# First attention as one stream of slots over four turns, with stacked fp32r score operands and the product by values ahead of the turns

## The chip, the core and the metric

The kernel runs on one core of a Trainium2 chip. A core has TensorE (PE: matrix products and transposes into PSUM), VectorE (DVE), ScalarE (ACT), GpSimd (POOL) and SyncE (SP, which here only issues DMAs). The metric is the device time of one execution in microseconds, as a median of several.

## The reference

Two layers over x of 8 sequences by 256 tokens by 256 numbers. Only the attention of layer 0 is touched by the change:

```python
xn = _layernorm(x)
q = heads(xn @ wq.T + bq); k = heads(xn @ wk.T + bk); v = heads(xn @ wv.T + bv)   # 32 heads of 8 numbers
scores = jnp.einsum('bhqd,bhkd->bhqk', q, k) / np.sqrt(8)
attn = softmax(where(causal, scores, -inf), axis=-1)
s = einsum('bhqk,bhkd->bhqd', attn, v).transpose(0, 2, 1, 3).reshape(B, S, H) @ wo.T + bo
g = silu(ffn0(xn));  x = x + s * g        # ffn0: router over 8 experts, top 2, and a shared expert
```

A second layer (another attention with 16 heads of 128, and 16 experts with top 4) follows; its text does not change.

## The kernel before

All is fp32 unless said otherwise. The first attention works on the 2048 tokens in four **turns** (`TURNS`) of 512, that is two sequences each. A turn has 32 **slots** (`SLOTS`): a slot is two heads of one sequence; `bb` is the sequence, 16 slots each. Queries and keys lie with the heads' 8 numbers along the partitions, so that 32 partitions hold four heads. The queries are `qT`; the keys are kept four times in `kTm`, each copy masked so that one head of each four is left (`keys`, L772: one DVE instruction for each copy), and a score product contracts over 32 partitions, 24 of them with zeros.

A slot's work goes over three engines, and each handles its own list in program order:

- **PE**, per slot (`scores`, L624, L626 and L630): products of queries and keys of two heads (256 and 128 columns, on two different groups of 32 partitions), and the causal mask added by a bf16 product with the identity. Two PSUM banks hold a slot's scores and two slots' scores alternate, so that `scores(s)` waits for the exponentials of slot s-2. Then `turn` (L640): six 128 by 128 transposes of the probabilities of slot s-2, through banks 4 and 5; each bank must have been copied out before it is written again. On every second slot `pv` (L659, L662): the product with the values for slots s-4 and s-3, which needs the copies of their transposed probabilities.
- **DVE**, per slot: the largest score of each row (L839, 256 wide, and L841, 512 wide), and then two copies of transposed probabilities of slot s-2 out of PSUM (L780).
- **ACT**, per slot: four exponentials with sums (L742, L744).

Beside these (`beside`) come side jobs at certain slots: the projection of values (L561), router logits (L568), the turning of the next turn's normalised tokens (L246), and in the third turn the router's choice and ranks (DVE L357 to L497, PE L440 and L443). At a **turn's end** the stream stops. PE drains the last turns and products, and then does `turn_inverse` (L673: the softmax's inverse sums turned), the projections of queries and keys for the next turn (L550), and the output projection `project` (L684), while DVE does `normalise` (L793), `keys` (L772) and `keep_out` (L799) and ACT `copy_out` and `queries` (L710). A new turn starts with `scores` of slot 0 once queries and the first four masked keys are there.

Of the other engines: POOL clears two large areas at the start (L2221, L2227), normalises, and in the last turn issues the 32 indirect DMAs (L502) that spread the tokens over the experts' rows. SP loads the constants, 1 MB of the second layer's weights, the shared and the eight experts' weights (4.9 MB in one DMA) and writes zeros to `xg` in 7 DMAs of up to 2 MB (L2132), all by the middle of turn 0. Behind the attention `pe_blocks0` (from L881) begins with the experts' blocks.

## Time and profile before

| | us |
|---|---|
| median of 3 runs (1939.71 to 1941.13) | 1941.01 |
| profiled execution: its time, and its span | 1924.45, 1922.6 |
| first attention: first slot of turn 0 to first product of the experts | 27.11 to 418.83 |
| busy between 36 and 418.8 us: PE, DVE, ACT, POOL | 364.19, 292.80, 231.68, 33.94 |
| DVE side jobs between 36 and 420: inverse sums (L784, L786), `normalise` (L793), `keep_out` (L799) | 7.7, 5.4, 5.5 (all four turns) |
| the same: normalising (L216, L221, L226); masked keys (L772) | 7.6 (three turns); 17.8 (24 instructions) |
| the same: router's choice, ranks and owners (L357 to L497) | about 9.7 (once) |
| an fp32r product of 512 columns (L1371), mean of one | 0.419 |

The rest of the time is the experts of layer 0 (to about 540 us) and the second layer. A row of the timeline is: start in us, duration in us (of a merged run of `xN` instructions, from the first's start to the last's end), engine, line, operation, result and operands, and in square brackets how long the engine had been idle and what released it. An fp32 product shows as two PE instructions, so `x4` in L624 is two products. The end of a product is modelled and lies some tenths of a us behind the moment at which the next one can start: what a group costs PE is read from start to start.

### The profile page before, as it was taken

The numbers are of one execution on the slowest core, as the hardware profiler recorded it, in microseconds if no ns is written. First come the engines' busy times: TensorE is split into PE (matmuls) and PEld (weight loads), VectorE is DVE, ScalarE is ACT, GpSimd is POOL, SyncE is SP. The second block draws the span as 40 slices with busy tenths as digits, with TensorE's granted clock in tenths as the row PEclk, the third lists the DMA queues.
The fourth block names the chain that finished last, engine by engine and source line by source line (L and its number), as shares of the span: only waits on it lengthen the run. The fifth ranks groups of instructions, "written<-read, shape, count | busy, mean of one in ns | idle before, by whom it ended". The sixth has DMA issues, their size and how long they took to land.

```text
span 1922.6 us, 34586 instructions
## 1 busy us (share of the span) xinstructions
PE 1815.3 (94%) x11822; PEld 1443.5 (75%) x11822; DVE 1282.4 (67%) x2811; ACT 906.2 (47%) x2978; POOL 832.7 (43%) x919
## 2 busy tenths in 40 slices
PE   6999999999987999999999999999999997999986
PEld 4767666767765887788888888888888886777754
DVE  5678787863457788888676766667667664444467
ACT  3657564753433444445454455544545543444422
POOL 2000000320056665565767767777676773000066
PEclk9899999999999999999999999999999998999999
DMA  9600000123342000000000000000000223333344
GB/s 345 231 1 2 1 1 1 59 90 112 90 158 94 1 1 12 1 6 1 15 20 14 19 16 14 19 14 11 25 11 22 77 78 136 106 108 107 105 132 123
DMA packets 75907, 114.29 MB, mean 59 GB/s; under 512 B 9505, under 2 KB 65953, under 8 KB 73089
## 3 DMA queue, kind: packets, MB, share of 16 engines
q1 hardware_dynamic: 66416, 86.38, 13.6%
q0 software_dynamic: 9216, 25.18, 4.0%
q8 instruction: 75, 1.23, 0.3%
q10 hardware_dynamic: 144, 1.05, 0.1%
q14 instruction: 56, 0.45, 0.1%
HBM read 64.86 MB, written 47.71 MB: 59 GB/s over the span
## 4 chain that ended last, share of the span: by engine, by line
PE 77%; DVE 10%; POOL 5%; issue 3%; ACT 3%; DMA 2%; POOLq 0%; DVEq 0%; SPq 0%; ACTq 0%
PE ps L1356 11%; PE ps L1371 9%; PE ps L1443 5%; PE ps L1889 5%; PE ps L1397 4%; PE ps L640 4%; PE ps L624 3%; PE ps L1385 3%; PE ps L1384 3%; PE ps L1383 3%; PE ps L902 2%; POOL work L2084 2%; PE ps L1378 2%; PE ps L1906 2%; PE ps L1908 2%
## 5 line engine op out<-in xcount | busy, mean ns | idle before, releaser
L1356 PE MATMUL ps<-work,weights 128*128 128x256 f32 x1024 | 248.3, 386 | 1.1 <-DVE work L1629 1.1
L1371 PE MATMUL ps<-split 128*128 128x512 f32 x768 | 227.8, 419 | 0.0
L1356 PEld LDWEIGHTS ps<-work,weights 128*128 128x128 f32 x1024 | 186.4, 191 | 22.1 <-DVE work L1629 1.3
L1771 POOL TENSOR_TENSOR work<-work,rope 128x512 f32<-128x512 f32 x128 | 164.5, 1286 | 53.1 <-ACT work L1544 53.0
L1777 POOL TENSOR_TENSOR work<-work 128x512 f32<-128x512 f32 x128 | 164.4, 1284 | 5.0
L502 POOL DMA_INDIRECT xg<-work x96 | 96.9, 1009 | 153.1 <-PE ps L630 140.2
L2084 POOL DMA_INDIRECT work<-yg,work x64 | 62.4, 975 | 227.1 <-DMA yg<-work 207.3
L742 ACT ACTIVATE work<-ps,work 128x128 f32<-128x128 f32 x256 | 95.4, 373 | 124.3 <-DVE work L841 117.4
L1371 PEld LDWEIGHTS ps<-split 128*128 128x128 f32 x768 | 130.9, 190 | 24.6
L780 DVE COPY work<-ps 128x384 f32<-128x384 f32 x256 | 130.0, 549 | 8.5 <-PE ps L640 8.4
L1443 PE MATMUL ps<-weights,work 128*128 128x256 f32 x512 | 124.0, 386 | 2.5 <-ACT work L1600 2.5
L640 PE MATMUL ps<-ident,work 128*128 128x128 f32 x768 | 116.5, 283 | 8.1 <-DVE work L780 8.0
L1651 DVE TENSOR_TENSOR work<-ps,keep_w 128x384 f32<-128x384 f32 x128 | 65.4, 553 | 87.1 <-PE ps L1379 86.8
L744 ACT ACTIVATE work<-ps,work 128x256 f32<-128x256 f32 x256 | 122.4, 478 | 0.0
L2021 DVE SCALAR_TENSOR_TENSOR work<-work,ps 128x176 f32<-128x176 f32 (+1 forms) x95 | 35.0, 369 | 121.5 <-ACT work L1972 121.5
L1585 ACT ACTIVATE work<-ps,work 128x128 f32<-128x128 f32 x256 | 90.6, 366 | 51.4 <-PE ps L1385 51.1
L1443 PEld LDWEIGHTS ps<-weights,work 128*128 128x128 f32 x512 | 99.4, 195 | 16.8 <-ACT work L1600 3.1
L1664 DVE RECIPROCAL work<-ps 128x256 f32<-128x256 f32 x64 | 111.9, 1748 | 0.0
L1550 ACT COPY work<-ps 128x256 f32<-128x256 f32 x128 | 47.1, 368 | 130.3 <-PE ps L1371 130.3
L1889 PE MATMUL ps<-weights,work 128*128 x316 | 106.8, 461 | 0.2 <-ACT work L1966 0.2
L1383 PE MATMUL ps<-work 128*128 128x64 f32 (+1 forms) x512 | 97.3, 272 | 9.1 <-DVE work L1651 9.1
L640 PEld LDWEIGHTS ps<-ident,work 128*128 128x128 f32 x768 | 88.1, 145 | 22.8 <-issue 11.5
(236 smaller groups left out, 4508.8 us busy)
## 6 DMA issues: line engine op xcount, KB each, us to landing
work<-xg SPq DMA_DIRECT2D x118, 128.0 KB, 2.2
yg<-work SPq DMA_DIRECT2D x118, 128.0 KB, 1.7
xg<-work SPq DMA_DIRECT2D x6, 2048.0 KB, 17.8
weights<-in_w SPq DMA_DIRECT2D x8, 1024.0 KB, 9.4
weights<-in_f SPq DMA_DIRECT2D x8, 1024.0 KB, 5.1
weights<-in_f SPq DMA_DIRECT2D x1, 4864.0 KB, 16.0
work<-xn SPq DMA_DIRECT2D x32, 128.0 KB, 2.2
weights<-in_wo SPq DMA_DIRECT2D x1, 2048.0 KB, 8.6
```

What stands on the lines that cost most here:

```text
L640: last = pe.transpose(ps[:, 4 + hh, k * P:(k + 1) * P], prob[:, s % RING, hh, k * P:(k + 1) * P], ident[:, :])
L744: act.activation(pr[:, P:BLK], sc[:, 0:SEQ], ACT.Exp, bias=nmax[:, s % RING, 1, hh:hh + 1], accum_out=total[:, bb, 1, h:h + 1]).then_inc(e ...
L780: dve.tensor_copy(probT[:, s % RINGT, hh, :], ps[:, 4 + hh, 0:BLK]).then_inc(probT_ready.sem, 1)
L1356: last = pe.matmul(ps[:, 2, which * SEQ:(which + 1) * SEQ], w1(h, (which * KC + kc) * P, P), xT[:, kc, :], start=kc == 0, stop=kc == KC - 1)
L1371: last = pe.matmul(ps[:, 3, :], x1_split[:, xp, kc, c * P:(c + 1) * P], w_vg[:, n % 2, wp, kc, :], start=i == 0, stop=i == KC * len(TERMS) ...
L1383: pe.matmul(outs[0], left[:, 0:P], rhs[0], start=True, stop=True)
L1443: last = pe.matmul(ps[:, 7, c * D:(c + 1) * D], ogT[:, hh, c * P:(c + 1) * P], weights[:, W1O + h * D:W1O + (h + 1) * D], start=h == 0 and ...
L1664: dve.reciprocal(enz[:, n % 2, :, :].rearrange("p c n -> p (c n)"), ps[:, 0, SEQ:2 * SEQ])\
L1771: pool.tensor_tensor(qk[:, h % 4, :, :], raw[:, h % 2, :, :], rope[:, 0, :].unsqueeze(1).broadcast_to([P, 2, SEQ]), ALU.mult).then_inc(rot ...
L1777: pool.tensor_tensor(qk[:, h % 4, :, :], qk[:, h % 4, :, :], rot_s[:, h % 2, :, :], ALU.add)\
L1889: last = pe.matmul(ps[:, 2 + b % 2, 0:GUW], xb4T[:, b % 2, kc * P:(kc + 1) * P], experts1[:, bass.ds(offset[b] + kc * GUW, GUW)], start=kc ...
L2084: pool.indirect_dma_start(out=yk4[:, c % 2, k, :], out_offset=None, in_=yg1[:, :], in_offset=bass.IndirectOffsetOnAxis(ap=route1.index[:, ...
```

## The change

What it does, part by part:

- The four turns become **one stream** of 128 slots (`ALL`), numbered g. The slot number within a turn is still s. All that stood at a turn's end is now a side job at some s, mostly odd: `lower_bank` and `upper_bank` on PE, `beside` on ACT and DVE. The results of `turn_inverse` and `project` use banks 6 and 7.
- **Scores as fp32r products.** ACT writes the projected queries and keys whole (`act_heads`), and `split_heads` splits each into an upper part (rounded to fp32r) and a lower part (the rest). On DVE for turn 0, on POOL for turns 1 to 3. SP writes these to DRAM (`write_halves`: 16 DMAs of 256 KB in a turn) so that for each head the 32 rows are upper-upper, upper-lower, lower-upper and lower-lower parts of its 8 numbers (queries take the first word, keys the second), and loads **stacks** back (`load_stack`: 16 DMAs of 256 KB in a turn, one for two slots, in a ring of 5). A score product contracts over these 32 rows in fp32r. The masked keys `kTm` are gone.
- **The product by values** (`pv`) stands right behind a slot's scores and ahead of the turns; before, it stood behind the turns.
- The zeros to `xg` go in 15 parts of up to 1 MB, one behind each of 15 stack loads of turns 0 and 1; experts' and shared weights, and the second layer's first 1 MB, are loaded in turn 2. `out_bias` and the ranks move to other slots; some semaphores are used again later.

The diff, cut to its core:

```diff
+FIRST = 15, 17
+ALL = TURNS * SLOTS
+RINGQ = 5
+PROJ = 2 * KC
...
+        def split_heads(eng, t, n):
+            index, ring = t * PROJ + n, n % 2
+            eng.wait_ge(full_ready.sem, full_ready.at(t, n + 1))
+            if index >= 2:
+                eng.wait_ge(halves_written[ring], 16 * 4 * (index // 2))
+            eng.tensor_copy(halves[:, ring, 0, :], full[:, ring, :]).then_inc(upper_ready.sem, 1)
+            eng.wait_ge(upper_ready.sem, upper_ready.at(t, n + 1))
+            eng.tensor_tensor(halves[:, ring, 1, :], full[:, ring, :], halves[:, ring, 0, :], ALU.subtract).then_inc(lower_ready.sem, 1)
...
+            def lower_bank(t, s):
+                if s == 1 and 0 < t < TURNS - 1:
+                    pe.wait_ge(full_ready.sem, full_ready.at(t, PROJ))
+                    logits(6)
+                if s == 1 and t == TURNS - 1:
+                    pe.wait_ge(full_ready.sem, full_ready.at(t, PROJ))
+                    pe.wait_ge(pow_rows, 7)
+                    route0.pe_rank(pe, 6)
+                if s == 21 and t < TURNS:
+                    turn_inverse(t, 0)
+                if s == 23 and t < TURNS:
+                    project(t, 0)
+                if t < TURNS - 1:
+                    if s == 25:
+                        pe.wait_ge(s0_ready.sem, s0_ready.at(t, 1))
+                        values(0)
+                    if s == 27:
+                        pe.wait_ge(v_ready.sem, v_ready.at(t + 1, HPQ))
+                        heads(t + 1, 2, 6)
+                    if s == 29:
+                        pe.wait_ge(full_ready.sem, full_ready.at(t + 1, 3))
+                        heads(t + 1, 3, 6)
...
+                    if s == FIRST[routed]:
+                        pe.wait_ge(norm0.xT_ready.sem, norm0.xT_ready.at(t + 1, 2))
+                        if routed:
+                            pe.wait_ge(lg0_copied.sem, lg0_copied.at(t + 1, 1))
+                        heads(t + 1, 0, 7)
+                    if s == FIRST[routed] + 2:
+                        pe.wait_ge(full_ready.sem, full_ready.at(t + 1, 1))
+                        heads(t + 1, 1, 7)
...
+            def scores(g):
+                n = g // 2
+                if g % 2 == 0:
+                    pe.wait_ge(stack_loaded[n % RINGQ], 16 * (n // RINGQ + 1))
+                if g >= 2:
+                    pe.wait_ge(exp_done.sem, exp_done.at(0, 2 * g - 2))
+                heads = [(2 * (g % 2) + hh, stack[32 * r:32 * r + 32, n % RINGQ, 0, :], stack[32 * r:32 * r + 32, n % RINGQ, 1, :])
                          for hh, r in enumerate(rows)]
 
                 for bank, q, k in heads:
-                    pe.matmul(ps[:, bank, 0:SEQ], q[:, q0 + P:q0 + SEQ], k[:, q0:q0 + SEQ], start=True, stop=True)
+                    pe.matmul(ps[:, bank, 0:SEQ], q[:, P:SEQ], k[:, 0:SEQ], start=True, stop=True)
...
-            for s in range(SLOTS + LAG + 1):
-                if s < SLOTS:
-                    scores(s)
-                    beside(s)
+            pe.wait_ge(norm0.xT_ready.sem, norm0.xT_ready.at(0, KC))
+            for n in range(PROJ):
+                heads(0, n, 2 + n)
+            values(0)
+            pe.wait_ge(consts_loaded, NCONST)
+            pe.wait_ge(bias_done, 5)
+            for g in range(ALL + 9):
+                t, s = divmod(g, SLOTS)
+                if g < ALL:
+                    scores(g)
+                if LAG < g <= ALL + LAG and (g - LAG) % 2 == 0:
+                    pv(g - LAG - 2)
+                lower_bank(t, s)
+                upper_bank(t, s)
                 for hh in range(2):
-                    if LAG <= s < SLOTS + LAG:
-                        turn(s - LAG, hh)
-                if s > LAG and (s - LAG) % 2 == 0:
-                    pv(s - LAG - 2)
...
+        def act_heads(act, t, n, bank):
+            which, mt = n % 2, n // 2
+            index = t * PROJ + n
+            act.wait_ge(proj_done.sem, proj_done.at(t, n + 1))
+            if index >= 2:
+                act.wait_ge(lower_ready.sem, lower_ready.at(0, index - 1))
+            act.activation(full[:, n % 2, :], ps[:, bank, :], ACT.Identity, bias=(bqs, BK)[which][:, mt:mt + 1],
+                           scale=(HD0 ** -0.5, 1.0)[which]).then_inc(full_ready.sem, 1)
...
-            def keys(turn, mt):
-                dve.wait_ge(k_done.sem, k_done.at(turn, mt + 1))
-                for j in range(HPQ):
-                    dve.tensor_scalar(kTm[:, j, mt, :], ps[:, 4 + mt, :], BK[:, mt:mt + 1], MASK[:, j:j + 1], ALU.add, ALU.mult)\
-                       .then_inc(keys_ready.sem, 1)
...
+            for g in range(ALL + 9):
+                if g < ALL:
+                    largest(g)
+                beside(*divmod(g, SLOTS))
+                if LAG <= g < ALL + LAG:
+                    copy_probs(g - LAG)
...
+            def write_halves(t, n):
+                which, mt, ring = n % 2, n // 2, n % 2
+                sp.wait_ge(lower_ready.sem, lower_ready.at(t, n + 1))
+                at = (t * KC + mt) * HPQ * P
+                rows = heads_by_part[at:at + HPQ * P, which * CH:(which + 1) * CH].rearrange("(h a b d) t -> a b h d t", a=2, b=2, d=HD0)
+                for a in range(2):
+                    for b in range(2):
+                        sp.dma_start(rows[a, b], halves[:, ring, (a, b)[which], :].bitcast(F32)).then_inc(halves_written[ring], 16)
+
+            def load_stack(n):
+                t, i = divmod(n, STACKS)
+                bb, mt, j = i // (KC * HPQ), i // HPQ % KC, i % HPQ
+                for w in range(2):
+                    sp.wait_ge(halves_written[w], 16 * 4 * (t * KC + mt + 1))
+                if n >= RINGQ:
+                    sp.wait_ge(scores_done.sem, scores_done.at(0, 4 * (n - RINGQ) + 4))
+                at = ((t * KC + mt) * HPQ + j) * P
+                sp.dma_start(stack[:, n % RINGQ, :, :].bitcast(F32),
+                             heads_by_part[at:at + P, :].rearrange("p (w t) -> p w t", w=2)[:, :, bb * SEQ:(bb + 1) * SEQ])\
+                  .then_inc(stack_loaded[n % RINGQ], 16)
...
+            for n in range(PROJ):
+                write_halves(0, n)
+                if n == 1:
+                    for i in range(HPQ):
+                        load_stack(i)
+            for i in range(HPQ, RINGQ):
+                load_stack(i)
+            for n in range(RINGQ, TURNS * STACKS):
+                t, i = divmod(n, STACKS)
+                if t < TURNS - 1 and i == 14:
+                    write_halves(t + 1, 0)
+                    write_halves(t + 1, 1)
+                if t and i == HPQ:
+                    write_halves(t, 2)
+                    write_halves(t, 3)
+                load_stack(n)
+                if 0 <= n - RINGQ - 2 < ZERO_PARTS:
+                    zero_rows(n - RINGQ - 2)
+                if t == 2 and i < E0:
+                    load_expert(i)
+                if t == 2 and i == E0:
+                    sp.dma_start(shared0, A["sh0"]).then_inc(f0_loaded, 16)
+                if t == 2 and i == E0 + 2:
+                    load_pair(0)
 ```

TensorE in the middle of turn 0, a pair of slots without side jobs. L624, L626 and L630 before, L689, L691 and L695 now, are a slot's scores; L640 and L705 the turns; L659 and L662, and L724 and L727, the product by values. Before:

```order
L624 MATMUL ps<-work 128x256 x2
L626 MATMUL ps<-work 128x128 x2
L630 MATMUL ps<-causal_b,ident_b 128x256 x2
L640 MATMUL ps<-ident,work 128x128 x6
L659 MATMUL ps<-work,weights 32x256 x4
L662 MATMUL ps<-work,weights 32x128 x4
L624 MATMUL ps<-work 128x256 x2
```

Now, in the same place:

```order
L689 MATMUL ps<-split 128x256 x2
L691 MATMUL ps<-split 128x128 x2
L695 MATMUL ps<-causal_b,ident_b 128x256 x2
L724 MATMUL ps<-work,weights 32x256 x4
L727 MATMUL ps<-work,weights 32x128 x4
L705 MATMUL ps<-ident,work 128x128 x6
L689 MATMUL ps<-split 128x256 x2
```

The scores' operands come from `split` (fp32r), and the product by values has moved ahead of the turns.

TensorE at a turn's end. Before, from the last scores of a turn to the first of the next (L673 turns the inverse sums, L550 projects queries and keys, L684 is `project`):

```order
L630 MATMUL ps<-causal_b,ident_b 128x256 x2
L640 MATMUL ps<-ident,work 128x128 x12
L659 MATMUL ps<-work,weights 32x256 x4
L662 MATMUL ps<-work,weights 32x128 x4
L640 MATMUL ps<-ident,work 128x128 x6
L659 MATMUL ps<-work,weights 32x256 x4
L662 MATMUL ps<-work,weights 32x128 x4
L673 MATMUL ps<-ident,work 128x128 x4
L550 MATMUL ps<-work,weights 128x512 x4
L673 MATMUL ps<-ident,work 128x128 x4
L550 MATMUL ps<-work,weights 128x512 x4
L684 MATMUL ps<-weights,work 128x256 x8
```

Now such a job stands between a slot's scores and its turns; here slots 15 and 16 of a turn, with the next turn's projection of queries (L573):

```order
L689 MATMUL ps<-split 128x256 x2
L691 MATMUL ps<-split 128x128 x2
L695 MATMUL ps<-causal_b,ident_b 128x256 x2
L573 MATMUL ps<-work,weights 128x512 x2
L705 MATMUL ps<-ident,work 128x128 x6
L689 MATMUL ps<-split 128x256 x2
L691 MATMUL ps<-split 128x128 x2
L695 MATMUL ps<-causal_b,ident_b 128x256 x2
L724 MATMUL ps<-work,weights 32x256 x4
L727 MATMUL ps<-work,weights 32x128 x4
L705 MATMUL ps<-ident,work 128x128 x6
```

SyncE at the start, behind the load of the rest of x. Before:

```order
L2122 DMA x_res<-in_x 128x12x256
L2112 DMA weights<-in_w 128x2048
L2124 DMA weights<-in_sh 128x2176
L2127 DMA weights<-in_f 128x9728
L2132 DMA xg<-work 128x16x256 x2
```

Now:

```order
L2185 DMA x_res<-in_x 128x12x256
L2194 DMA heads_by_part<-split 16x8x512 x8
L2204 DMA split<-heads_by_part 128x2x256 x4
L2194 DMA heads_by_part<-split 16x8x512 x8
L2204 DMA split<-heads_by_part 128x2x256 x3
L2214 DMA xg<-work 128x8x256
```

The first scores wait for eight writes to DRAM and one load back; the large loads stand behind.

## Rows read from the trace of the kernel before

**Rows 1.** TensorE in a pair of slots, timeline

```profile
184.87 0.70 PE L624 MATMUL ps<-work 32*128 32x256 f32 x4
...
185.72 0.39 PE L630 MATMUL ps<-causal_b,ident_b 128*128 128x256 bf16 x2
185.98 0.98 PE L640 MATMUL ps<-ident,work 128*128 128x128 f32 x6
186.89 0.64 PE L659 MATMUL ps<-work,weights 128*32 128x256 f32 x8
...
187.68 0.70 PE L624 MATMUL ps<-work 32*128 32x256 f32 x4
...
189.51 0.70 PE L624 MATMUL ps<-work 32*128 32x256 f32 x4
```

**Rows 2.** That pair by windows: stretch, length, busy of each engine, clock, DMA

```profile
184.87:189.51 4.64, 4.64 (x49) 3.32 (x48) 3.83 (x9) 3.91 (x17) 0.00 (x0) 1.00 0.00 0
```

**Rows 3.** VectorE and what it waits for in turn 0, timeline

```profile
113.84 0.41 DVE L839 TENSOR_REDUCE work<-ps 128x2 f32<-128x256 f32 x1
...
114.17 0.68 DVE L841 TENSOR_REDUCE work<-ps 128x2 f32<-128x512 f32 x1
...
114.77 1.01 DVE L780 COPY work<-ps 128x384 f32<-128x384 f32 x2
...
118.22 0.98 PE L640 MATMUL ps<-ident,work 128*128 128x128 f32 x6 [1.02 <-DVE work L780]
...
118.78 1.02 DVE L780 COPY work<-ps 128x384 f32<-128x384 f32 x2 [0.24 <-PE ps L640]
```

**Rows 4.** TensorE at first slots of turns and at turn ends, timeline

```profile
27.11 0.70 PE L624 MATMUL ps<-work 32*128 32x256 f32 x4
...
133.84 0.70 PE L624 MATMUL ps<-work 32*128 32x256 f32 x4
...
222.42 3.60 PE L550 MATMUL ps<-work,weights 128*128 128x512 f32 x8
225.85 3.62 PE L684 MATMUL ps<-weights,work 128*128 128x256 f32 x16
229.40 0.70 PE L624 MATMUL ps<-work 32*128 32x256 f32 x4
...
333.00 0.70 PE L624 MATMUL ps<-work 32*128 32x256 f32 x4
...
406.65 0.70 PE L624 MATMUL ps<-work 32*128 32x256 f32 x4
...
418.83 0.60 PE L881 MATMUL ps<-ident,work 128*128 128x128 f32 x4
```

**Rows 5.** An fp32r product of the second layer, timeline

```profile
902.85 0.96 PE L1371 MATMUL ps<-split 128*128 128x512 f32 x3
```

**Rows 6.** The start: first queries on ACT, timeline

```profile
22.07 0.69 ACT L710 ACTIVATE work<-ps,bqs 128x512 f32<-128x512 f32 x1 [2.75 <-PE ps L550]
```

**Rows 7.** The page on DMAs: line, count, KB each, us from issue to landing

```profile
work<-xn SPq DMA_DIRECT2D x32, 128.0 KB, 2.2
```

**Rows 8.** Issues on SyncE at the start, timeline

```profile
9.42 0.43 SPq L2121 DMA_DIRECT2D first_row<-in_first_row  x1
```

**Rows 9.** Granted clock by windows, columns as in rows 2

```profile
40.00:42.00 2.00, 2.00 (x12) 1.46 (x10) 1.97 (x6) 0.00 (x0) 0.00 (x0) 0.50 1.09 385
301.00:304.00 3.00, 2.43 (x22) 1.48 (x22) 2.75 (x6) 2.81 (x14) 0.00 (x0) 0.62 0.00 0
316.00:319.00 3.00, 1.99 (x26) 1.17 (x24) 2.76 (x7) 1.72 (x8) 0.00 (x0) 1.00 0.00 0
```

**Rows 10.** TensorE around the third turn's ranks and at 64 us, timeline

```profile
64.37 1.22 PE L624 MATMUL ps<-work 32*128 32x256 f32 x4
...
67.77 1.23 PE L624 MATMUL ps<-work 32*128 32x256 f32 x4
...
301.57 1.37 PE L640 MATMUL ps<-ident,work 128*128 128x128 f32 x6 [2.31 <-DVE work L780]
```

More of the change, by code:

```diff
@@ L584, in beside, with upper_bank @@
+            def upper_bank(t, s):
+                if t == 0:
+                    if s == 1:
+                        logits(7)
+                    if s == 3:
+                        pe.wait_ge(lg0_copied.sem, lg0_copied.at(0, 1))
+                        bias_row()
+                else:
+                    if s == 5:
+                        turn_inverse(t - 1, 1)
+                    if s == 7:
+                        project(t - 1, 1)
+                if s == 9 and t < TURNS:
                     if t:
@@ L2230, in _ @@
                 norm0.pool_all(pool, t)
+                for n in range(PROJ):
+                    split_heads(pool, t, n)
             pool.wait_ge(xg_zeroed, 16 * ZERO_PARTS)
```

469 lines of the change are left out of this document (225 added, 244 removed).

## The prediction

> **What bounds the kernel now.** I read first the timeline of TensorE in the middle of a turn. In a pair of slots TensorE goes from start to start through scores (184.87 to 185.98), turns (to 186.89), product by values (to 187.68), scores and turns again (to 189.51) [rows 1]: 4.64 us, and the windows view shows it busy for all 4.64, VectorE for 3.83 and ScalarE for 3.91 [rows 2]. So TensorE's issue is the bound, with VectorE only 0.4 us per slot behind it. Then the turn ends: three turns start at 133.84, 229.40 and 333.00, after 106.7, 95.6 and 103.6 us, and the last, with its end, takes 85.8 [rows 4]. Sixteen pairs are 16 x 4.64 = 74 us, so in turn 1 some 21 us are side jobs and the turn's end, in which the other engines mostly stand. Turn 0 has windows in which the clock is 0.50 although TensorE is busy all the time [rows 9]; one slot there takes 3.40 us from 64.37 to 67.77 [rows 10], against 1.83 for the same slot at 187.68 [rows 1], 1.85 times as much. Turn 2 carries the router.
>
> **Scores in fp32r.** In a slot the fp32 products take 185.72 - 184.87 = 0.85 and the mask 0.26 [rows 1]. No row shows an fp32r product on 32 partitions. Bounds: an fp32 product is two instructions; an fp32r product is one, and one of 512 columns comes about every 0.27 us ((0.96 - 0.42) / 2, with the 0.42 of one alone from the table) [rows 5]. Lower bound: a quarter of 0.85, if time goes by columns and passes: 0.21 + 0.26 = 0.47. Middle bound: half of it, if time goes by instructions: 0.43 + 0.26 = 0.69. Upper bound: nothing gained, 1.11. I take 0.63, nearer to the second: 0.27 for 512 columns is near a rate by columns, but with 128 and 256 columns what each instruction costs by itself weighs more. That is 0.48 less per slot, 61 us of TensorE's work over 128 slots.
>
> A rule speaks for the dearer side. Eight loads and products of scores take 0.85, or 0.106 each [rows 1]. The Trainium skill, "TensorE: Matmul & The Clock Gate", section "LDWEIGHTS (loading the stationary operand)": a load takes its columns over 1.2 ns, however few its rows, so 0.107 for 128 columns. The trace agrees, if loads are what counts. By that, the four fp32r products are estimated at 0.43 and the slot's scores at 0.69; 0.06 more in each of 62 slots of pairs with a long side job would make the result 4 us longer.
>
> **A plain pair, now.** Two slots' scores 1.26, product by values 0.79, turns 2 x 0.75 (the second slot's 1.83 less its scores leaves 0.72 [rows 1]; I take 0.75): 3.55 on TensorE. But VectorE needs 3.83 [rows 2] and becomes the bound, and the new order makes it wait. The product by values needs the last copy of the slot before. Behind that copy TensorE needs 0.06, then 0.79 for the product, then the first three transposes, whose copy starts 0.56 after them (118.22 to 118.78) [rows 3]: 1.41 us. VectorE finds its next largest scores ready and needs only 0.33 + 0.60 = 0.93 for them (113.84, 114.17, 114.77) [rows 3]. So it stands for 0.48 us once a pair. Pair: 1.41 + copies 0.98 (half of 3.83 less 0.93) + 0.93 + 0.98 = 4.30 us, against 4.64. With the turns first that 0.48 would not be there.
>
> **Pairs with a side job.** The jobs of a turn's end are now side jobs of odd slots. Half of L550 with 8 instructions is 3.43 / 2 = 1.72, half of `project` 3.55 / 2 = 1.78 [rows 4]; I put values, logits, projections, `project` and ranks all at 1.75. Jobs of four transposes or the bias row are small, 0.5. In a pair with a large job TensorE is the bound: 3.55 + 1.75, and a wait: the product by values needs the copies of transposes that stand only one scores block before it. From the first transpose 0.56, copies 0.98 and 0.06, 1.60, against 0.75 + 0.63 = 1.38 that TensorE has to do: 0.22, say 0.25. Sum 3.55 + 1.75 + 0.25 = 5.55. A small job makes 3.55 + 0.5 + 0.25 = 4.30 on TensorE, as long as VectorE's chain; I take 4.4.
>
> - Turn 0: 8 large 44.4, 4 small 17.6, 4 plain 17.2: 79.2. VectorE's side jobs (table) are some 8 us a turn, mostly in pairs with a large job, where it has 5.55 - 3.83 to spare; what is left I put at 2.5, and 3 in the others: 81.7. Half clock: it cost turn 0 about 106.7 - 95.6 = 11 us; with cheaper work, 9. Sum 90.7.
> - Turn 1: 9, 4 and 3: 50.0 + 17.6 + 12.9 + 3 = 83.5.
> - Turn 2: 10, 4 and 2: 55.5 + 17.6 + 8.6 + 3 = 84.7, and of the router's 9.7 us on VectorE (table) six fall here, half of them covered: 87.7.
> - Turn 3: 4, 2 and 10: 22.2 + 8.8 + 43.0 + 3, and 3 for ranks and owners: 80.0. This turn is longer than its 76.0 before (333.00 to 406.65 and one slot of 2.32), since it takes over the end of turn 2.
>
> `keys` on VectorE, 17.8 us, is gone; it lay in the turn's end, which is counted whole.
>
> **Start.** The first scores need splits, eight writes and one load. The first queries reach ScalarE at 22.07 [rows 6]; keys come 1.72 later, 23.8, ScalarE 0.69, two VectorE instructions about 1.1 (0.43 for a 512-wide copy of L786, 0.69 as L793): 25.7. SyncE issues a DMA every 0.43 us or so [rows 8]; the keys' four go out behind the queries' four at 27.6, land 2.2 to 2.5 later (2.2 for 128 KB [rows 7]), and the load needs as much: 33. First slot at 33 instead of 27.11 [rows 4]. The values lie inside this wait. Bounds: 30.5 with everything overlapped, 38 if 256 KB in many rows lands at twice the 2.2.
>
> **End.** From the end of slot 31 (406.65 + 2.32) to the experts' first transposes (418.83) [rows 4] are 9.9 us. The chain stays: exponentials, turns, copies, product, inverse, `project` of one sequence. Unchanged, 9.9.
>
> **Hidden.** The splits on POOL have nothing else beside them. 32 DMAs a turn on SyncE are 14 us of issuing in some 85. Stacks are in a ring of five, so that a load is issued four pairs, 17 us, ahead, and the zeros' parts between them don't reach that. The later chain is that of the second keys: made at slot 29, split, written (four issues, 1.8, and 2.3), needed as a stack at slot 8 of the next turn, 11 slots or 24 us later. If a cover fails, all three engines wait.
>
> **Sum.** 33 + 90.7 + 83.5 + 87.7 + 80.0 + 9.9 = 384.8 against 418.8: 34 us less on a profiled execution of 1924.45. The median of the runs is 16.6 us above that execution; I take the same difference off it: 1941 - 34 = **1907 us**.
>
> **The rivals.**
> - *More overlap than I allow.* The 0.48 and 0.25 waits vanish, plain and small pairs cost VectorE's 3.83, large ones 5.30, side jobs of VectorE are covered (2 us each left for the router in two turns), and turn 0 keeps its clock: 73 + 74 + 78 + 69 + 33 + 9.9 = 337, 82 us less: 1859. For it: engines have slots of slack. Against: two score banks, and the waits are in every plain pair.
> - *fp32r on 32 rows costs what fp32 did* (1.11): slower. 0.96 more in 31 large pairs, 0.8 in 14 small, 0.5 in 19 plain: 50 us on top, 1957. It decides from 0.63 + 0.48 x 34 / 50 = 0.96 us a slot. Against: [rows 5].
> - *The clock falls.* With shorter products and a wait in every pair TensorE may run at 0.50. After 2.31 us idle at 301.57 [rows 10] the window shows 0.62; but at 316 to 319 it was busy 1.99 of 3.00 and kept 1.00 [rows 9]. At half clock a large pair is 1.85 x 5.30 + 0.25 = 10.1, a small one 7.7, a plain one 6.8: 4.5 x 31 + 3.3 x 14 + 2.5 x 19, the whole stream 234 us more. It decides from a seventh of the stream; a third gives some 1980. The Trainium skill, same page, section "A second HAM failure mode: psum-queue depth-cycling", tells of short idle times between groups of products that make the clock go to and fro; by that, this rival would come true in part.
> - *Stacks come late at the turn's change*, some 5 us at three changes: 1922.
>
> **How the numbers follow.** Forecast 0.50, more overlap 0.18, dear fp32r 0.10, clock 0.12, late stacks 0.10. The range reaches up into the rivals with dear scores and a fallen clock, 1950, and down to half of the way to full overlap and a little beyond, 1868. Outside are about 0.1 on each side. Faster by over 0.2% (3.9 us, about what a measurement of this kernel can tell from no change): the forecast, more overlap, late stacks and a part of the others, 0.79; within, 0.05; slower 0.16.
>
> **What would show it.** First scores near 33 us; a pair without side jobs at 4.3 us with VectorE waiting about 0.5 us for transposes in it; pairs with a projection near 5.5; turns of about 91, 83, 88 and 80 us; a slot's scores 0.63 from start to start. It is wrong if scores take over 0.96, if windows of 0.50 fill more than turn 0's, or if TensorE waits for stack DMAs.

## The result: 0.5% faster, where 1.8% was forecast

The changed kernel takes 1931.5 us (median of 5 runs, 1928.5 to 1931.8), the kernel before 1941.0 beside it. The ratio is 0.9946, with a 95% interval of 0.9928 to 0.9965. Forecast were 1907 us in a range of 1868 to 1950: the time lies in the range and the sign is right, but of the 34 us only 9.5 came.

The profiled execution of the changed kernel took 1931.79 us, with a span of 1930.0. First the profile's page: TensorE's and the others' busy times, and the queue that carries instructions (queue, kind: packets, MB, share of 16 engines):

```profile
PE 1778.7 (92%) x11310; PEld 1406.8 (73%) x11310; DVE 1272.5 (66%) x2787; ACT 908.8 (47%) x2986; POOL 855.8 (44%) x943
...
q8 instruction: 107, 1.75, 0.4%
```

The 512 PE instructions less than before (11310 against 11822) are the second instructions of the scores' 512 fp32 products. The prediction did not speak of the queue of instructions. It turns out to be the row that matters.

Next a plain pair of slots near the end of the stream, TensorE's timeline, which answers to [rows 1]:

```profile
368.48 0.38 PE L689 MATMUL ps<-split 32*128 32x256 f32 x2
368.70 0.22 PE L691 MATMUL ps<-split 32*128 32x128 f32 x2
368.85 0.39 PE L695 MATMUL ps<-causal_b,ident_b 128*128 128x256 bf16 x2
369.08 0.86 PE L705 MATMUL ps<-ident,work 128*128 128x128 f32 x6
369.87 0.38 PE L689 MATMUL ps<-split 32*128 32x256 f32 x2
...
371.29 0.64 PE L724 MATMUL ps<-work,weights 128*32 128x256 f32 x8 [0.65 <-DVE work L827]
371.74 0.40 PE L727 MATMUL ps<-work,weights 128*32 128x128 f32 x8
372.08 0.87 PE L705 MATMUL ps<-ident,work 128*128 128x128 f32 x6
372.88 0.39 PE L689 MATMUL ps<-split 32*128 32x256 f32 x2
```

The scores of a slot take 0.60 us (368.48 to 369.08), forecast 0.63. The pair takes 4.40 (368.48 to 372.88), forecast 4.30. TensorE stands for 0.65 us ahead of the product by values, since the copies on VectorE aren't done. VectorE in the same pair answers to [rows 3]:

```profile
371.48 0.68 DVE L907 TENSOR_REDUCE work<-ps 128x2 f32<-128x512 f32 x1
372.66 1.02 DVE L827 COPY work<-ps 128x384 f32<-128x384 f32 x2 [0.50 <-PE ps L705]
```

There is the wait that the prediction named: 0.48 worked out, 0.50 measured. Over the whole first attention the waits view gives

```profile
DVE work L827 <- PE ps L705: 52.3, 75, 1.6
```

and the same view for TensorE:

```profile
PE ps L724 <- DVE work L827: 30.7, 40, 3.4
PE ps L689 <- DMA split<-heads_by_part: 7.1, 1, 7.1
```

(engine, waiting line, what it waited for: us in total, times, longest). In this pair each of the two engines waits for the other once; over the 64 pairs VectorE waits 75 times and TensorE 40 times. For a stack of queries and keys TensorE waited once only, for the first. The starts of the turns and of the experts, TensorE's timeline, answer to [rows 4]:

```profile
36.30 0.58 PE L689 MATMUL ps<-split 32*128 32x256 f32 x2 [7.10 <-DMA split<-heads_by_part]
...
118.40 0.38 PE L689 MATMUL ps<-split 32*128 32x256 f32 x2
...
205.56 0.38 PE L689 MATMUL ps<-split 32*128 32x256 f32 x2
...
294.80 0.38 PE L689 MATMUL ps<-split 32*128 32x256 f32 x2
...
388.77 0.60 PE L938 MATMUL ps<-ident,work 128*128 128x128 f32 x4
```

So the first attention with its start ends at 388.8 us. Before, it was 418.8 [rows 4]: 30 us are gained there, and 9.5 are left at the end of the kernel.

**Where the rest went.** I cut the span at two rows: the first transposes of the first layer's experts (L881 before, L938 after), and the last product of the second layer's heads (L1356 before, L1419 after). For the two profiled executions at hand, and then for both kernels from the experiments:

| us | to the experts | from there to the last L1356 / L1419 | rest | span |
|---|---|---|---|---|
| before | 418.8 | 1177.8 | 326.0 | 1922.6 |
| after | 388.8 | 1195.8 | 345.4 | 1930.0 |
| before_again | 420.0 | 1181.4 | 343.4 | 1944.8 |
| after_again | 389.8 | 1193.5 | 326.7 | 1910.0 |

The third column goes with the chip and not with the kernel: the eight profiles of the second and third group of experiments, on two chips, have 326 to 328, and the four of the first group, on a third, 341 to 343. The 16.6 us between the profiled execution of before and its median agree with this, and setting the forecast off from the median was right. The second column goes with the kernel: 1178 to 1181 before, 1194 to 1196 after. There the change touches no instruction, and there 12 to 18 us are lost. Against the forecast of 1907 the 24.5 us too many are, on these two profiles (together 24.8), 4.0 of the first attention, 18.0 of the second column, and 2.8 by which the third differs by more than the 16.6 allowed for.

The waits of TensorE from 900 to 1600 us, after (before has no such row for its products):

```profile
PE ps L1460 <- issue: 11.1, 4, 3.1
```

and the place of one of them in the timeline:

```profile
1001.41 2.33 PE L1460 MATMUL ps<-work 64*128 64x256 f32 x16 [2.86 <-issue]
```

"issue" says that TensorE waited for nothing that the profile shows. The four waits stand one loop pass (some 126 us) apart in the second layer's loop over sequences, `with pe.Fori(2, SEQ_END)`. After this wait the granted clock is lower, as the windows view shows (columns as in [rows 2]):

```profile
1000.00:1004.00 4.00, 2.59 (x18) 2.19 (x18) 0.24 (x1) 0.10 (x2) 1.44 (x3) 0.76 0.02 5
1004.00:1008.00 4.00, 4.00 (x24) 3.67 (x23) 2.44 (x7) 2.03 (x5) 1.16 (x2) 0.81 0.00 0
```

My theory at this point: TensorE's instructions of the loop no longer stay where the engine reads them, and are fetched again in each pass, because the changed first attention is 962 instructions shorter (TensorE's compiled program has 18,319 instructions instead of 19,281) and the loop's 1637 instructions have moved by that much. Its rivals: that the fetches come and go from run to run, or that the loss comes from the clock or from something else that the first attention leaves behind.

### The profile page after: what moved, and what is told of

It is laid out like the page before. It is cut to its first block, busy times and chain, and to the rows that moved or that the text cites. A ratio compares the mean times of both kernels' runs of the same rounds, so it can differ in the third digit from the quotient of the medians.

```text
span 1930.0 us, 34158 instructions
## 1 busy us (share of the span) xinstructions
PE 1778.7 (92%) x11310; PEld 1406.8 (73%) x11310; DVE 1272.5 (66%) x2787; ACT 908.8 (47%) x2986; POOL 855.8 (44%) x943
## 3 DMA queue, kind: packets, MB, share of 16 engines
q8 instruction: 107, 1.75, 0.4%
q10 hardware_dynamic: 144, 1.05, 0.1%
## 4 chain that ended last, share of the span: by engine, by line
PE 73%; DVE 12%; issue 6%; POOL 4%; DMA 2%; ACT 2%; another core or an unknown queue 1%; SPq 0%; POOLq 0%; DVEq 0%; ACTq 0%
PE ps L1419 11%; PE ps L1434 9%; PE ps L1506 5%; PE ps L1952 5%; PE ps L1460 4%; DVE work L827 4%; PE ps L705 3%; PE ps L1448 3%; PE ps L1447 3%; PE ps L1446 3%; PE ps L959 2%; PE ps L724 2%; PE ps L1441 2%; PE ps L1969 2%; PE ps L1971 2%
## 5 line engine op out<-in xcount | busy, mean ns | idle before, releaser
L827 DVE COPY work<-ps 128x384 f32<-128x384 f32 x256 | 130.8, 550 | 53.1 <-PE ps L705 52.3
L705 PE MATMUL ps<-ident,work 128*128 128x128 f32 x768 | 115.7, 289 | 0.4 <-DVE work L827 0.4
L1460 PE MATMUL ps<-work 64*128 64x256 f32 (+1 forms) x1024 | 103.1, 342 | 12.6 <-issue 11.1
L705 PEld LDWEIGHTS ps<-ident,work 128*128 128x128 f32 x768 | 90.7, 148 | 24.0 <-issue 20.3
## 6 DMA issues: line engine op xcount, KB each, us to landing
heads_by_part<-split SPq DMA_DIRECT2D x64, 256.0 KB, 4.0
split<-heads_by_part SPq DMA_DIRECT2D x64, 256.0 KB
work<-xg SPq DMA_DIRECT2D x118, 128.0 KB
yg<-work SPq DMA_DIRECT2D x118, 128.0 KB, 1.7
```

Source lines behind the costliest of these rows:

```text
L705: last = pe.transpose(ps[:, 4 + hh, k * P:(k + 1) * P], prob[:, g % RING, hh, k * P:(k + 1) * P], ident[:, :])
L827: dve.tensor_copy(probT[:, g % RINGT, hh, :], ps[:, 4 + hh, 0:BLK]).then_inc(probT_ready.sem, 1)
L1460: last = pe.matmul(ps[:, 4 + hh, at], k[rows, half, keys], q[rows, half, queries], start=half == 0, stop=half == 1)
```

## The experiments

All ratios below are to the kernel before on the same chip. Medians of different chips differ (before: 1945.1 on one, 1923.0 on the other), so times are compared within a group.

### First group: the loop's place, and the order within a slot

**before_again**, the kernel before, not changed.

> The kernel before, unchanged, with a new profile. Its profiled execution took 1924.45 us, 16.6 under the median of 1941, and I took the same difference off the forecast. Code theory (TensorE's instructions are fetched again in every pass of the second layer's loop where the loop lies badly in the instruction stream): the same kernel always lies the same way, so no packets of the instruction queue between 1002 and 1528 us, about 75 packets in all, and a time of 1941 if the execution differs from the median in something else, which a profile near 1941 would show. Rival (the fetches come and go from run to run): a profile near 1941 has about 30 packets more and a wait of some 3 us at the head of each pass.

Measured: 1943.7 us, profiled 1946.56, with

```profile
q8 instruction: 75, 1.23, 0.3%
```

75 packets, as the code theory says, though the execution took 22 us longer than the one that I had read. The difference is in the last section (343.4 against 326.0) and 4 us of it in the middle. The rival that fetches come and go falls. The row gives a size too: 1.23 MB in 75 packets are 16.4 KB each, and 1.23 MB for 19,281 instructions are 64 bytes each, so a packet brings 256 instructions and the whole program is fetched once.

**before_shift** adds met waits to the kernel before, at the head of TensorE's program (two of them become one instruction):

```
-            pe.wait_ge(first_loaded, 16 * len(first_loads))
+            for _ in range(125):
+                pe.wait_ge(first_loaded, 16 * len(first_loads))
             norm0.pe_all(pe, 0)
```

> The kernel before with 62 more instructions (waits that are already met) at the head of TensorE's program, where TensorE stands for about 15 us anyway: the loop's start then lies at the same place within 256 instructions as in the changed kernel. Code theory: the loop is fetched again in each pass, about 30 packets of the instruction queue more, TensorE waits some 3 us per pass at the loop's first product, half clock behind it, and the kernel takes 15 to 25 us more than before. Rival (it is the first attention's change or the clock that costs later on): within 2 us of before and no further packets.

Measured: 1956.4 us, ratio 1.0081 (1.0052 to 1.0110). The queue on the page, and TensorE's waits in the loop:

```profile
q8 instruction: 111, 1.82, 0.4%
```

```profile
PE ps L1397 <- issue: 11.1, 4, 2.9
```

36 packets more, and the same four waits of together 11.1 us, in a kernel whose work is that of before to the last product. The middle section takes 1197.9 us instead of 1181.4. So the loss needs nothing of the first attention but its length in instructions. The net loss is 13 us, a little under the 15 to 25 expected and smaller than these 16.5: the experts start at 414.3 instead of 420.0. The first attention's text is the same in both, but in before_again TensorE stood at half clock for 20.5 us of it and here for 6.8 (windows of 2 us), and it took 386.0 us instead of 391.5. So a few us of difference between two executions can be the clock's.

**after_shift** puts 194 such instructions into the changed kernel, at the same place (389 waits).

> The changed kernel with 194 more such instructions at the same place, so that its loop starts at the place within 256 instructions that the kernel before has. Code theory: about 72 packets of the instruction queue instead of 107, no wait of 3 us at the loop's head, about 1931 - 20 = 1911 us, so that most of the missing gain is back. Rival: 1931, the shift does nothing.

Measured: 1925.5 us, ratio 0.9906 (0.9884 to 0.9929), 72 packets, and no such wait. My number of 1911 was missed, and the trace says by what: the padding itself delays the head.

```profile
L251 PE MATMUL ps<-ident,work x64: 270/273/445, 29.3 to 1467.6; 128*128 128x128 f32 x64
```

The first transposes start at 29.3 us instead of 15.6, and the experts at 403.3 instead of 388.8, 14.5 later. The middle section is 1181.0, as in before. The loss in the loop is gone, and nearly as much was paid at the start.

**turns_first** takes the product by values behind the turns, as before the change:

```
-                if LAG < g <= ALL + LAG and (g - LAG) % 2 == 0:
-                    pv(g - LAG - 2)
                 lower_bank(t, s)
                 upper_bank(t, s)
                 for hh in range(2):
                     if LAG <= g < ALL + LAG:
                         turn(g - LAG, hh)
+                if LAG < g <= ALL + LAG and (g - LAG) % 2 == 0:
+                    pv(g - LAG - 2)
```

> The changed kernel with one thing undone: in a slot the turns come ahead of the product by values again, so the product does not stand between a slot's scores and the transposes that VectorE waits for. By the sum of the prediction VectorE's wait of 0.48 us in each plain pair goes (19 pairs, 9 us) and the 0.25 in 45 others (11 us): 10 to 20 us less, 1912 to 1921. Rival (the product's own wait for VectorE's copies, behind which TensorE stands now, only moves to the turns, since VectorE's work of 3.83 us a pair is the bound): within 3 us of the changed kernel. A third way: slower, because the copies that the product needs are now those of the same slot's turns one pair before, and scores wait behind it.

Measured: 1907.9 us, ratio 0.9818 (0.9796 to 0.9841), against 0.9946 for the changed kernel on its chip: by the ratios some 25 us less, a little beyond the 10 to 20; the two intervals together leave about 6 us either way. The second group prices it on one chip. It still has the 107 packets. The rival that the wait only moves falls.

### Second group: both causes at once, and the scores by themselves

**after_again** is the changed kernel on the chip of this group.

> The changed kernel unchanged, beside its variants: 1931 to 1936 us, with 107 packets of the instruction queue. It is there so that the others are compared on one chip.

Measured: 1911.4 us, ratio 0.9937 (0.9924 to 0.9951). The absolute number expected was that of another chip; the ratio agrees with 0.9946, and the packets are 107.

**after_fit** pads by 104 instructions, at two places where TensorE stands anyway:

```
+            for _ in range(125):
                 pe.wait_ge(first_loaded, 16 * len(first_loads))
             norm0.pe_all(pe, 0)
...
             values(0)
+            for _ in range(85):
+                pe.wait_ge(consts_loaded, NCONST)
```

> The changed kernel with 104 instructions more ahead of the loop on TensorE, all of them waits that are already met, 62 at the head of the program and 42 between the first values and the first scores, where TensorE stands for 7 us anyway. (The 194 at the head alone made the first transposes start at 29.3 us instead of 15.6, which took back most of what the loop gained.) Code theory: about 72 packets, scores still from 36 us, and the 14 us that the second layer took longer than before between the first experts' start and its last product are gone: 1917 us. Rival (the position decides it only where it is equal to that of before, 63 or so past a multiple of 256, and 229 is bad too): 107 packets or more and 1931.

Measured: 1896.0 us, ratio 0.9858 (0.9841 to 0.9874), 15.4 us less than after_again. The queue on the page; the two lines at which I cut the span, each with its first and last start; and the windows at 1000 us:

```profile
q8 instruction: 71, 1.16, 0.3%
```

```profile
L939 PE MATMUL ps<-ident,work x110: 272/273/477, 390.9 to 576.6; 128*128 128x128 f32 x110
...
L1420 PE MATMUL ps<-work,weights x1024: 377/379/634, 590.3 to 1571.3; 128*128 128x256 f32 x171
```

```profile
996.00:1000.00 4.00, 4.00 (x20) 3.48 (x20) 2.48 (x5) 1.66 (x5) 3.05 (x4) 1.00 0.00 0
1000.00:1004.00 4.00, 4.00 (x31) 3.12 (x31) 2.70 (x4) 1.70 (x7) 3.40 (x3) 1.00 0.01 2
```

The middle section is 1180.4 us (390.9 to 1571.3) instead of 1193.5, and the granted clock around 1000 us, where the loop returns here too, stays at 1.00. Expected were 14 us less, which is what came; the 1917 was again a number of the other chip. That the loop need not lie where it lay before, but only outside of a bad stretch, holds too.

**turns_first_fit** has both edits.

> Both together: turns ahead of the product by values, and the 104 instructions. If the two costs are independent, 1908 - 14 = 1894 us. Rival (the same waits are counted twice): 1900 or more.

Measured: 1873.5 us, ratio 0.9742 (0.9727 to 0.9757): 22.5 less than after_fit and 37.8 less than after_again. Expected were 14 + 23 = 37 us less than the changed kernel (1931 to 1894), so the two costs add up. This version is faster than both kernels of the case, 2.6% against the 0.5% of the change as it was made. A plain pair in it:

```profile
349.97 0.38 PE L689 MATMUL ps<-split 32*128 32x256 f32 x2
...
352.40 0.98 PE L705 MATMUL ps<-ident,work 128*128 128x128 f32 x6 [0.16 <-DVE work L828]
353.32 0.64 PE L724 MATMUL ps<-work,weights 128*32 128x256 f32 x8
353.77 0.40 PE L727 MATMUL ps<-work,weights 128*32 128x128 f32 x8
354.10 0.38 PE L689 MATMUL ps<-split 32*128 32x256 f32 x2
```

4.13 us instead of 4.40, and the product by values (353.32) starts at once. VectorE's wait for transposes over the first attention, after_fit and then turns_first_fit:

```profile
DVE work L828 <- PE ps L705: 53.9, 76, 2.1
```

```profile
DVE work L828 <- PE ps L705: 19.7, 25, 1.0
```

76 waits have become 25. The first attention ends at 369.0 instead of 390.9. Not all of this need be the order's: TensorE stood at half clock for 28.8 us of the first attention here and for 46.3 in after_fit. Between turns_first (42.0) and after_shift (42.7), on one chip, that time is the same, and there the first attention is 15 us shorter (338.5 against 353.5). So about 15 us are the order at the same clock, and the rest of the 22.5 goes with less time at half clock; whether the order brings that about isn't shown.

**after_f32** reads the same stacks as fp32:

```
-                heads = [(2 * (g % 2) + hh, stack[32 * r:32 * r + 32, n % RINGQ, 0, :], stack[32 * r:32 * r + 32, n % RINGQ, 1, :])
+                heads = [(2 * (g % 2) + hh, stack[32 * r:32 * r + 32, n % RINGQ, 0, :].bitcast(F32), stack[32 * r:32 * r + 32, n % RINGQ, 1, :].bitcast(F32))
```

> The changed kernel with the scores' products read as fp32 instead of fp32r, nothing else; the loop lies as in the changed kernel. The prediction's price for it: 1.11 a slot instead of 0.63, 0.96 more in 31 large pairs, 0.8 in 14 small and 0.5 in 19 plain, 50 us: 1981. Rival (VectorE bounds the pairs, so that TensorE's longer scores are partly covered): 25 to 35 us more, about 1960. A second rival (short fp32r products are what lowers the clock in the first turn): well under 1960, with the granted clock at 0.98.

Measured: 1955.9 us, ratio 1.0170 (1.0155 to 1.0185), 44.5 more than after_again (1981 and 1960 were numbers of the chip on which the changed kernel takes 1931; here they would be 50 and some 30 more than 1911); by the two profiles the first attention ends 49.1 us later (438.9 against 389.8). One slot's scores:

```profile
412.25 0.70 PE L689 MATMUL ps<-split 32*128 32x256 f32 x4
412.78 0.39 PE L691 MATMUL ps<-split 32*128 32x128 f32 x4
413.10 0.39 PE L695 MATMUL ps<-causal_b,ident_b 128*128 128x256 bf16 x2
413.33 0.82 PE L705 MATMUL ps<-ident,work 128*128 128x128 f32 x6
```

1.08 us (412.25 to 413.33) instead of 0.60. So the rival "fp32r on 32 rows costs what fp32 did" was sized right, 50 us by the sum and 44.5 to 49 measured, and it isn't what happens. Some 4 of the 49 can be the clock's, since TensorE stood at half clock for 55.0 us of this first attention against 42.1. The rival that VectorE would cover a third to a half of it falls, and so does the one that short fp32r products lower the clock: the mean granted clock is 0.973 here and 0.976 in after_again. And without fp32r the whole change would have made the kernel 1.7% slower.

### Third group: which places are bad

Four times the kernel before with other numbers of waits at the head (65, 207, 277 and 637 instead of 125). Each ran once, beside a single run of before (1922.9 us): 1925.5, 1953.7, 1963.6 and 1967.6 us. They are there for the packets and the middle section and not for the time, since the waits delay the start in part.

**pos95**

> The kernel before with 32 instructions more at the head of TensorE's program (met waits): its loop starts 95 past a multiple of 256 instructions. So far: 63 and 229 good (71 to 75 packets of the instruction queue), 125 bad (107 and 111). The loop has 1637 instructions, 6.4 blocks of the 256 that one packet of 16.4 KB brings. Block theory: what decides is whether the loop touches 7 blocks or 8, so that the bad places are one stretch of about 100 of the 256, which begins between 64 and 125. 95 is open by it: 75 packets or 111, nothing between.

**pos166**

> The same with 103 instructions, start at 166. Block theory: bad (111 packets) if the bad stretch begins behind 66, good only if it begins at 64 to 66; so bad is expected. Rival (a bad place is a matter of one or two places only): 75 packets.

**pos201**

> The same with 138 instructions, start at 201. Block theory: bad if the stretch begins behind 101, and then 95 is good; good if it begins before that. It may not be that 95 and 201 are both bad, since these lie 106 apart: that would refute the theory.

**pos125_256**

> The same with 318 instructions, 256 more than in the kernel that was fetched again in each pass, start at 125 once more. Block theory (only the place within a block of 256 counts): 111 or 112 packets, so bad again, though the loop lies a whole block later. Rival (what counts is the absolute place or the time at which the loop is reached): 75.

Measured, with the earlier kernels in the same table (start of the loop in TensorE's compiled program, modulo 256; the program of before is itself four packets longer than the changed one; turns_first, after_again and after_f32 start at 125 too, turns_first_fit at 229):

| start | kernel | packets | waits at L1397 / L1460, us | middle section, us |
|---|---|---|---|---|
| 63 | before_again | 75 | none | 1181.4 |
| 63 | after_shift | 72 | none | 1181.0 |
| 95 | pos95 | 75 | none | 1180.8 |
| 125 | before_shift | 111 | 11.1 | 1197.9 |
| 125 | after | 107 | 11.1 | 1195.8 |
| 125 | turns_first | 107 | 11.0 | 1193.9 |
| 125 | after_f32 | 111 | 10.5 | 1192.9 |
| 125 | pos125_256 | 112 | 11.4 | 1194.2 |
| 166 | pos166 | 111 | 11.5 | 1200.0 |
| 201 | pos201 | 111 | 22.9 | 1212.4 |
| 229 | after_fit | 71 | none | 1180.4 |
| 229 | turns_first_fit | 71 | none | 1177.8 |

Where the place is good, the packets are as many as the program has whole blocks of 256 instructions (75 for before's 19,281, 71 for after_fit's 18,423); where it is bad there are 36 more each time, nine for each of the loop's four returns.

pos201 is the dearest of them, by TensorE's waits:

```profile
PE ps L1397 <- issue: 22.9, 4, 6.1
```

Four waits of up to 6.1 us, and 31 us in the middle section. Why they are twice as long as at the other bad places isn't shown.

What is shown: the place modulo 256 decides, and a whole block of 256 more changes nothing. The bad places measured fit one stretch that begins between 96 and 125 and ends between 201 and 228, so that it is 77 to 133 long. A loop of 1637 instructions touches 7 blocks of 256 from 156 of the 256 places within a block and 8 from the other 100, which fits that length. It doesn't fit by the places of the compiled program as they are: counted so, the loop that starts at 125 touches 7 blocks and is bad, and the one at 229 touches 8 and is good. The block theory holds only if the blocks begin 31 to 54 instructions away from where the compiled program counts them, and no run shows why they should. The Trainium skill, "Runtime: NRT & Kernel Launch", section "Instruction fetch mechanics", says that TensorE holds 128 KiB of instructions, 2048, and refills in blocks of 16 KiB, and that a taken branch to a target outside the current window of two pages forces a fetch. The block size agrees with the 16.4 KB per packet here. The window of two pages does not agree: at the good places the loop goes back over more than six blocks, four times, without one packet more than the program has whole blocks, and the measurement decides. By the skill's size of 2048 instructions 8 blocks would just fit. If the block theory holds, a loop that touches 8 is fetched again in every pass and one that touches 7 is not; why the eighth wouldn't stay isn't shown, and that it is taken by the block fetched ahead is my guess.

## Why the prediction was too good by 24 us

By its own steps, forecast against the profiled execution of after:

| step | forecast | measured |
|---|---|---|
| scores of a slot | 0.63 | 0.60 |
| plain pair | 4.30 | 4.40 |
| VectorE's wait in it | 0.48 | 0.50 |
| first scores | 33 | 36.3 |
| turn 0 | 90.7 | 82.1 |
| turn 1 | 83.5 | 87.2 |
| turn 2 | 87.7 | 89.2 |
| turn 3 and end | 89.9 | 94.0 |
| experts' first transposes | 384.8 | 388.8 |
| everything behind it | unchanged | 12 to 18 longer |

- **The pairs and their waits** were right, and so was the price of fp32r: after_f32 gave 44.5 to 49 us for what the prediction had at 50. A slot's scores took 0.60, so its dearer estimate of 0.69, with 0.107 for each load and product, did not come: four of them take 0.37 us (368.48 to 368.85), 0.09 each.
- **The waits that the new order adds** were right. The terms 0.48 in 19 plain pairs and 0.25 in 45 others are 20 us; undoing them gave 22.5 to 25, about 15 of it at the same clock. This part of the change costs time, and the prediction had it inside its forecast.
- **The turns** were each off by 2 to 9 us, and their sum by 0.7: 351.8 forecast, 352.5 measured. Turn 0 was too dear by 8.6: I gave it 9 us for half clock, and it ran at half clock for 10 us where turn 0 of before had 24. Turns 1 and 3 were too cheap, and they had half clock for which I gave nothing (below). That the sum fits so well is partly luck.
- **The start** was mis-sized by 3.3 us. I let SyncE issue a DMA in 0.43 us [rows 8]; these write 128 rows each and take 0.73 (5.85 / 8, SyncE's timeline):

```profile
24.06 5.85 SPq L2194 DMA_DIRECT2D heads_by_part<-split  x8
...
33.13 2.53 SPq L2204 DMA_DIRECT2D split<-heads_by_part  x4
```

  The eight are out at 29.9 instead of 27.6, and the loads that wait for them start at 33.13, 3.2 us later and not 2.2 to 2.5; the first scores follow another 3.2 us later, at 36.30. The issue on [rows 8] was of another shape.
- **"The rest unchanged" is the step that failed.** It stood in the sum without a line of its own: the 34 us of the first attention went to the end of the kernel with nothing taken off. The second layer's loop is the same code, and yet took 15.7 us more (1193.5 against 1177.8 on alike profiles), because it lies at another place in TensorE's program. With the loop moved off the bad stretch alone (after_fit) the change is worth 27 us, 1923.0 to 1896.0, close to the 28 to 30 of the first attention. That could have been asked from the profile of before: its instruction queue shows 75 packets of 16.4 KB, one for every 256 instructions of the program and so none for the loop's repeated passes, which says that the loop fits, and with 6.4 blocks of 256 in it, not by much. Where the limit lies only the runs showed. No rival named it.
- **The rivals.** More overlap did not come: TensorE and VectorE go on waiting for each other. Late stacks did not come: there is one wait for a stack, the first. The clock rival came true in part. Its sign, windows of 0.50 (the lower of TensorE's two levels, 1.2 GHz) beyond turn 0's, is there. Turns 0 and 1 whole, and then a window each of turns 1 and 3 (columns as in [rows 2]):

```profile
36.30:118.40 82.10, 76.69 (x668) 53.80 (x668) 65.87 (x140) 59.20 (x269) 14.75 (x13) 0.94 0.84 277
118.40:205.56 87.16, 82.33 (x721) 56.82 (x720) 70.75 (x150) 60.38 (x273) 8.77 (x10) 0.92 0.48 154
126.00:128.00 2.00, 2.00 (x19) 1.16 (x20) 0.80 (x2) 1.11 (x6) 0.33 (x1) 0.50 0.69 201
304.00:306.00 2.00, 2.00 (x19) 1.16 (x20) 0.85 (x2) 1.05 (x5) 1.70 (x2) 0.50 0.19 70
```

  In the 2 us ahead of 126 TensorE was busy for 1.57. Summed over windows of 2 us (what a window lacks of 1.00, twice, times its length), TensorE was at half clock for 10, 14, 7 and 10 us of turns 0 to 3, and before for 24, 0, 3 and 0:

| first attention, us | length | of it at half clock |
|---|---|---|
| before, before_again, before_shift | 391.7, 391.5, 386.0 | 27.3, 20.5, 6.8 |
| pos95, pos166, pos201, pos125_256 | 389.1, 391.5, 387.2, 389.0 | 20.4, 20.5, 13.7, 20.4 |
| after, after_again, after_shift, after_fit | 352.5, 354.2, 353.5, 354.9 | 40.8, 42.1, 42.7, 46.3 |
| turns_first, turns_first_fit | 338.5, 333.2 | 42.0, 28.8 |
| after_f32 | 402.9 | 55.0 |

  41 of 352 us are a ninth of the stream, and the rival decides from a seventh. An estimate of what it costs: the seven executions with the first attention of before go from 386.0 us with 6.8 of it to 391.7 with 27.3, 0.3 for each us; so 41 us cost some 12, where the forecast had 9 and all of them in turn 0. The Trainium skill's section that the prediction cited on short idle times ("TensorE: Matmul & The Clock Gate", "A second HAM failure mode: psum-queue depth-cycling") would have the clock go to and fro in the first attention, and the trace agrees to that extent: it falls and rises again in each of turns 1 to 3. That the short waits are the cause isn't shown.

What the loop lost adds up: against the profile of before the middle section is 18.0 us longer, of which the four waits are 11.1, and TensorE is at half clock in it for 27 us instead of 17 (windows of 4 us), three times behind such a wait. At 0.3 for each us, or 0.46 by the slot of [rows 10] that took 1.85 times as long at half clock, that is an estimate of 3 to 5 more; 2 to 4 are left, as much as the good places differ among themselves (1177.8 to 1181.4). What stays open is why the last section takes 326 to 328 us on two chips and 341 to 345 on others, with all kernels alike. Its waits view has rows in before_again that before lacks, put down to "remote" (another core or an unknown queue), the largest 18.3 us of ScalarE's L1984.

## What to carry to other kernels

A kernel with a loop has a cost that no engine's work shows: whether the loop's instructions stay loaded, which depends on the number of instructions ahead of it. Before a change to the code ahead of a large loop, count packets of the instruction queue and compare them with the length of the program; after it, count again, and if packets appear in every pass, move the loop by some tens of instructions, at a place where the engine stands anyway. And when one edit holds a part that gains and a part that costs, price each by itself: here the fp32r scores were worth 45 us and the moved product cost 23. The version with the one and not the other is 1.8% faster than before instead of 0.5%, and with the loop off the bad stretch as well 2.6%. By these numbers an estimate for what is left of the change, the one stream and the stacks with fp32 scores and the old order, is only 5 us: 1955.9 less 15.4 and 22.5 is 1918, against 1923.0.

## What the runs showed of the hardware

- The same loop of 1637 instructions on TensorE is fetched once, or again in each pass, by its place modulo 256 instructions. The price was 10.5 to 22.9 us of waits in four returns, 12 to 31 us in all.
- Met waits are cheap only while the engine stands: 62 instructions of them at the head cost nothing (first transposes at 15.8 us). With 103, 138, 194 and 318 the first transposes start at 19.5, 23.3, 29.3 and 42.9 us (pos166, pos201, after_shift, pos125_256): 0.109 us for each instruction more. At 0.109 each the 42 that after_fit has behind the first values are 4.6 us, inside the 7 that TensorE stands there.
- A write of 128 rows of 2 KB to DRAM took SyncE 0.73 us to issue, against 0.43 for the one in [rows 8], and landed a median of 4.0 us behind its issue (the profile's page on DMAs, columns as in [rows 7]):

```profile
heads_by_part<-split SPq DMA_DIRECT2D x64, 256.0 KB, 4.0
```

- Two fp32r products of 256 columns on 32 rows go by in 0.22 us (368.48 to 368.70), the same two as fp32, four instructions, in 0.53 (412.25 to 412.78). With 128 columns it is 0.15 against 0.32. So at these sizes fp32r costs under half (0.42 and 0.47 of it), and the middle bound of the prediction, by instructions, was too dear.
